# A fused four-layer graph network on one core: stacked keys, staging and value products of the attention layer rewritten

## The reference

```python
Q = (x @ Wq + bq).reshape(Bs, Ns, 4, 32)          # K and V alike
scores = einsum('bnhd,bmhd->bhnm', Q, K) / sqrt(32)
scores = scores + (1.0 - adj[:, None, :, :]) * -1e9
attn = softmax(scores, axis=-1)
out = einsum('bhnm,bmhd->bnhd', attn, V).reshape(Bs, Ns, 128)
return out @ Wo + bo
```

## Time and profile before

| | |
|---|---|
| median of three runs | 13284.21 us |
| the profiled execution | 13291.54 us |
| its span (first to last instruction) | 13289.7 us |
| PE, PEld busy | 95%, 47% |
| DVE, ACT busy | 74%, 72% |
| mean granted TensorE clock | 0.972 |
| PE products of the second layer (L1017) | 7128.7 us |

### The profile page before, as it was taken

One profiled execution on the slowest core, in us unless ns is written; L12 is line 12 of the kernel. 1 busy time (PEld: TensorE's weight loads), 2 busy tenths in 40 slices (PEclk: granted clock), 3 DMA queues, 4 the chain that ended last, 5 costly groups with the idle time before them and its releaser, 6 DMA issues.

```text
span 13289.7 us, 251470 instructions
## 1 busy us (share of the span) xinstructions
PE 12572.4 (95%) x110721; PEld 6215.5 (47%) x110721; DVE 9769.1 (74%) x13975; ACT 9628.7 (72%) x8953; POOL 351.3 (3%) x500
## 2 busy tenths in 40 slices
PE   8998999989999899998999989999899998999989
PEld 3333843338433384333843338433384334843348
DVE  4887748877488774887758877588765887658876
ACT  4886748867488664886648866488664886658866
POOL 1000000000000000000000000000000000000000
PEclk9999999999999999999999999999999999999999
DMA  1001210012100121001310013100130001300022
GB/s 71 17 20 45 100 60 17 20 45 104 56 17 20 48 105 52 17 20 48 110 47 18 19 48 117 40 20 17 52 122 32 20 17 52 129 25 20 17 55 87
DMA packets 126941, 647.66 MB, mean 49 GB/s; under 512 B 15264, under 2 KB 49824, under 8 KB 52128
## 3 DMA queue, kind: packets, MB, share of 16 engines
q1 hardware_dynamic: 92688, 420.78, 9.4%
q0 software_dynamic: 20880, 143.66, 2.9%
q10 hardware_dynamic: 12288, 67.13, 2.2%
HBM read 556.01 MB, written 8.39 MB: 42 GB/s over the span
## 4 chain that ended last, share of the span: by engine, by line
PE 88%; DVE 6%; ACTq 2%; DMA 2%; ACT 1%; issue 1%; POOL 0%; SPq 0%; DVEq 0%
PE ps L1017 50%; PE ps L1001 10%; PE ps L1059 8%; PE ps L1072 4%; PE ps L1030 4%; PE ps L1050 3%; PE ps L1189 3%; ACTq L540 2%; PE ps L953 2%; DMA adj_ring<-in_adj 1%; PE ps L1177 1%; DVE E L678 1%; DVE E L679 1%; DVE PT L705 1%; DVE stats L604 1%
## 5 line engine op out<-in xcount | busy, mean ns | idle before, releaser
L1017 PE MATMUL ps<-E,a_win 128*32 128x512 f32 x65536 | 7128.7, 594 | 46.4 <-ACT E L439 34.9
L1017 PEld LDWEIGHTS ps<-E,a_win 128*32 128x32 f32 x65536 | 2114.9, 110 | 4879.7 <-issue 4737.3
L439 ACT ACTIVATE E<-Q,ka 128x2048 f32<-128x2048 f32 x2048 | 4073.1, 1989 | 0.0
L678 DVE TENSOR_SCALAR E<-Q,kd 128x2048 f32<-128x2048 f32 x2048 | 2631.1, 1285 | 1016.5 <-PE ps L1017 982.4
L438 ACT ACTIVATE E<-Q,ka 128x1280 f32<-128x1280 f32 x2048 | 2786.7, 1361 | 810.9 <-PE ps L1017 786.0
L679 DVE TENSOR_SCALAR E<-Q,kd 128x2048 f32<-128x2048 f32 x2048 | 2623.9, 1281 | 0.0
L746 DVE CUSTOM_DVE_ANT_0 T<-ps,adj_ring 128x2048 f32<-128x2048 f32 x512 | 1173.5, 2292 | 231.9 <-PE ps L1050 205.3
L680 DVE TENSOR_SCALAR E<-Q,kd 128x768 f32<-128x768 f32 x2048 | 1258.8, 615 | 0.0
L464 ACT ACTIVATE T<-T,nmin 128x2048 f32<-128x2048 f32 x512 | 1022.0, 1996 | 319.4 <-issue 199.3
L374 ACT ACTIVATE PT<-ps 128x512 f32<-128x512 f32 x1792 | 999.7, 594 | 287.3 <-PE ps L1059 275.4
L1059 PE MATMUL ps<-ident,T 128*128 128x128 f32 x8192 | 1129.8, 281 | 10.1 <-ACT PT L374 5.9
(11 more groups left out here) (119 smaller groups left out, 7558.4 us busy)
## 6 DMA issues: line engine op xcount, KB each, us to landing
adj_ring<-in_adj SPq DMA_DIRECT2D x384, 1024.0 KB, 4.9
adj_res<-in_adj POOLq DMA_DIRECT2D x128, 1024.0 KB, 7.4
qst<-qh ACTq DMA_DIRECT2D x64, 256.0 KB, 7.9
qst<-ql ACTq DMA_DIRECT2D x64, 256.0 KB, 9.0
kst<-kh ACTq DMA_DIRECT2D x64, 256.0 KB, 5.7
kst<-kl ACTq DMA_DIRECT2D x64, 256.0 KB, 5.9
HW<-in_x POOLq DMA_DIRECT2D x9, 1024.0 KB, 13.3
X<-in_x SPq DMA_DIRECT2D x128, 64.0 KB, 2.0
```

Of the source, the lines that this page charges most:

```text
L439: nc.scalar.activation(E[:, s + 3, :], Q2[:, :], ACT.Relu, bias=ka[:, u, 48 + m:49 + m]).then_inc(e_act, 1)
L678: nc.vector.tensor_scalar(E[:, s, :], Q2[:, :], kd[:, u, m:m + 1], 0.0, ALU.add, ALU.max)
L1017: last = mm(ps[QROWS * grp:QROWS * (grp + 1), 4 * u + c, :], win, E[:, s + grp, c * CH:(c + 1) * CH], start=(m == 0), stop=(m == QUADS - 1 ...
```

## The change

- **Stacking by PE.** The weights of Q and K are loaded four times side by side (`wq_r`, `wk_r`: head h's 32 columns repeated on 128), so one product gives head h's keys on all four partition groups (`fill`). ACT writes the rounded (high) value to all of them, and DVE overwrites the groups that shall hold the low part with the difference (`low`). The 32 staging DMAs of a batch are gone. Only tiles 0 and 1 of the queries are made that way. For tiles 2 to 15, Q is formed once (high part in `AGG`, low part in `HT`) and SP stacks each tile by 16 DMAs of 16 KB (`stack_queries`), two to four tiles ahead.
- **Order.** 28 `fill`s go through PSUM banks 4 to 7 and the first four steps' scores stand between them.
- **Values.** A step takes one quarter (4 key blocks) of all four heads of a tile, instead of all 16 blocks of one head. The four heads' products stand on the four column groups and accumulate in one bank, so nothing is left to combine. The probabilities of a tile are therefore transposed when its four heads are done: group `q` in step `q + 5`. Three banks (4, 5, 6) rotate.
- **Output.** For each tile, DVE spreads the reciprocal sums, PE transposes them (`spread2`), DVE multiplies them onto the result (`attend2`), PE multiplies by `Wo` (`output2`), DVE adds to `X`, and the statistics, the layer norm and the relu of the fourth layer follow for groups of tiles, all within the loop. POOL folds `dinv` into `rstd`.
- **Constants.** 30 small loads instead of 16 ahead of the first work.

The core of the diff (PE; then SP):

```diff
-            def values2(r, h, g, first):
...
-                for k in range(TPC):
-                    last = mm(ps[HD * k:HD * (k + 1), 6 + h % 2, 0:P], V[:, g * TPC + k, h * HD:(h + 1) * HD],
-                              PT2[:, g, k * P:(k + 1) * P], start=(g == 0), stop=(g == NC - 1),
-                              tile_position=(0, HD * k))
...
-                mm(ps[:, 6 + h % 2, P:P + HD], o4[:, h % 2, :], sel[:, :], start=True, stop=True).then_inc(c2_ps, 1)
...
+            def probs_t2(b, q, h):
+                t, g = q // NC, q % NC
+                if g == 0 and h == 0:
+                    pe.wait_ge(p2_rdy, b * STEPS + (t + 1) * HEADS)
...
+            def values2(b, q):
...
+                for k in range(TPC):
+                    for h in range(HEADS):
+                        last = mm(ps[HD * h:HD * (h + 1), 7, 0:P],
+                                  V[:, g * TPC + k, h * HD:(h + 1) * HD], PT2[:, q % 2, h, k * P:(k + 1) * P],
+                                  start=(g == 0 and k == 0), stop=(g == NC - 1 and k == TPC - 1),
+                                  tile_position=(0, HD * h))
...
+            def step2(b, s):
+                q = s - 5
+                if 0 <= q < GROUPS:
+                    for h in range(HEADS - 1):
+                        probs_t2(b, q, h)
+                if 0 <= q - 1 < GROUPS:
+                    values2(b, q - 1)
+                if 0 <= q < GROUPS:
+                    probs_t2(b, q, HEADS - 1)
+                if s % HEADS == 2 and 0 <= s // HEADS - 2 < NT:
+                    spread2(b, s // HEADS - 2)
+                if s % HEADS == 3 and 0 <= s // HEADS - 2 < NT:
+                    output2(b, s // HEADS - 2)
+                if s < STEPS:
+                    scores2(b, s)
...
+            def stack_queries(b, t):
+                sp.wait_ge(f_free, b * FILLS + 5 * HEADS + NC + t // TPC + 1)
+                if t >= 4:
+                    sp.wait_ge(s2_ps, b * STEPS + (t - 3) * HEADS)
+                for blk, part in enumerate((AGG, HT, AGG, HT)):
+                    for h in range(HEADS):
+                        sp.dma_start(qcur[HD * blk:HD * (blk + 1), t % 4, h, :].bitcast(F32),
+                                     part[HD * h:HD * (h + 1), t * P:(t + 1) * P]).then_inc(q_in[t % 4], 16)
```

## The result

The changed kernel takes 12977.9 us (median of 4 runs, 12970.25 to 12991.6), the kernel before 13285.44 (4 runs, 13282.43 to 13297.99). The ratio is 0.9761 [0.9748, 0.9774]: 2.4% faster. Forecast were 13040 with 12950 to 13180, so the direction and the range hold, and the forecast was 62 us too high.

A forecast was written before the change was run, and what follows sets the result against it. PE was taken to bound the kernel, with 28.06 us waiting for staging. Per batch 42.5 + 15 x 17.03 + 3 + 20.8 = 321.8 instead of 354.8; 13291.5 - 264 + 12 = 13040 us, range 12950 to 13180.

The forecast's parts named there:

- Start, 42.5 per batch: Attention layer's start: from first transposes to the transposes of group 0, 42.5 us without any DMA wait, bounds 41.5 to 46.
- Tile, 17.03: Attention loop: one tile lasts 17.03 us, the same as 4 x 4.265 = 17.06 before.
- The four legs: Loop, round a tile: fourth head's minimum to transposes 4.48, to scores 2.92, to next scores 3.84, by DVE to minimum 5.79.
- The 3 us set aside for the small pieces: Tile's fourth step, where DVE sets the pace: statistics, layer norm, relu and adding `bo`, 3 us per batch.
- The cause of the wait: Loop: a tile's transposes need all four heads' exponentials, 5.86 us against 3.73 of PE work, so PE waits once per tile.
- no new wait: Rival, loop: exponentials done within one PE step, 15.5 us per tile, 185 us less, total 12855; chance 0.08.
- The DVE leg: Ring's last leg, scores to the fourth head's minimum: by DVE with mask, copy and add 5.79 us; by PE 5.57.
- End, 20.8: Attention layer's end: from the transposes of step 65 to the fourth layer's first product, 20.8 us.
- Query DMAs, 0.48 per issue: SP's queue in the loop: 16 DMAs per tile at 0.48 us, 7.7 of a tile's 17 us, taken as covered.
- Constants, 12 once: Kernel start: 14 more constants delay the adjacency loads, 12 us once.
- The clock: Rival, loop: PE at half clock in the step behind the wait, 2.92 us more per tile, total 13390; chance 0.03.
- The others keep their durations: Fourth layer and the other layers: durations unchanged, they only start earlier.

The follow-up runs named there:

- Experiment 2: The kernel before, with the 16 staging DMAs of the keys issued by SP while ACT issues those of the queries: 13377.9 us, ratio 1.0056.
- experiment 7: The kernel before, staging only the first of four partition groups, scores contracting over its 32 partitions without the low parts: 13396.7 us, ratio 1.0083.
- experiment 1: The changed kernel, with PE waiting ahead of a head's first transposes for that head's exponential alone, not all four: 12850.7 us, ratio 0.9659.
- experiment 9: The changed kernel, with DVE making the next tile's mask in the tile's third step instead of its fourth: 12983.9 us, ratio 0.9775.
- Experiment 5: On top of experiment 1, DVE copies the last aggregate's transposes, needed by the fourth layer's first product, ahead of the last normalisations: 12818.9 us, ratio 0.9651.
- experiment 4: The changed kernel, with 32 query DMAs of 8 KB per tile instead of 16 of 16 KB: 13616.1 us, ratio 1.0237.
- 6: On top of Experiment 5, the 16 DMAs of replicated weights and biases moved behind the first batch's `x` loads in SP's queue: 12805.2 us, ratio 0.9642.

## Why the prediction was right, point by point

- **The bound** (PE, and its 28.06 us behind the staging). Right. Experiment 2 shows the staging bound by the DMA engines, and 7 that a quarter of it would have brought only 14 of the 28 us in the second batch, 11.4 in the mean. To gain all of it, the stacking by PE also had to take the scores out from behind the load of the next `x` and its statistics, a second wait which the prediction did not see. Nor was the DMA that ended PE's wait the last one, as the prediction read it: ACT issued further ones until 2965.0, 8 us after the first scores.
- **Start, 42.5 per batch.** 43.8 (41.5 in the last batch, and down to 40.3 in experiment 1, by the clock at the start). DVE's new form took 0.76 alone and 0.69 in a row instead of 0.62, inside the bounds 0.57 and 0.8.
- **Tile, 17.03.** This is the term with the largest miss. Without a piece of the statistics or the layer norm in its fourth step a tile took 16.65; with one, 16.90. The four legs, priced at 4.48, 2.92, 3.84 and 5.79, took 4.46, 2.86, 3.94 and 5.64 in the tile shown, and its DVE leg holds such a piece of 0.26: without it 5.38. The rows were read as lengths, but from start to start the pieces are shorter (mask 1.14, copy 0.58, add 0.20), and from the scores to the minimum are 1.22 instead of 1.38. The output product, priced as 0.46, took 0.22 from its start to that of the scores. PE's wait, put at 1.5, is 1.31 and stands 120 times. The 3 us set aside for the small pieces were the right pieces, but came to half: six times 0.25. Together 251.8 instead of 258.5, 6.7 per batch too much.
- **The cause of the wait.** Shown by experiment 1, which takes it away and saves 127 us. The rival "no new wait", 12855, was rightly given a small chance for the code as it stands; experiment 1 makes it the case and measures 12850.7. That the two agree within 5 us is partly luck: the tile was 15.6, not 15.5, and the start and the end differ from their prices.
- **The DVE leg.** Present: 0.26 us more or less on it moves the tile by 0.25. But "5.57 by PE" as the alternative beside 5.79 was too narrow a comparison: experiment 9 shows that the two neighbouring legs share DVE's work, and shortening one lengthens the other.
- **End, 20.8.** 21.8. The list of pieces was right, but the normalisation of three blocks and both relus, 1.4 us, stand ahead of the copies on DVE. Experiment 5 shows that this order, not the dependency, cost 2.4 us per batch.
- **Query DMAs, 0.48 per issue.** Too low: 0.63 in the median, 0.68 in the mean. They are covered, as forecast, with 11 of 16.9 us used; landing takes 2.7 and 2.2 us against 2.0. The warning of the Trainium skill's page "DMA: Bandwidth & Descriptors", section Bandwidth, about small transfers did not bite at 16 KB, and in experiment 4, at 8 KB, the number of issues bound, not the bytes.
- **Constants, 12 once.** 10.1 (first product at 57.14 instead of 47.05).
- **The clock.** 0.98 over the layer instead of 0.92, 1.00 in the loop: no half clock behind a wait of 1.3 us. At the start half the clock was there, as the prediction had it: 0.61 over the first 16 us.
- **"The others keep their durations."** Nearly. From a batch's first product to the attention layer's first transposes all eight batches took 9579.2 us instead of 9588.9, and the fourth layer 817.5 instead of 808.9. Two small errors of opposite sign cancel. No experiment was aimed at the fourth layer, and yet it took 779 to 825 us in sum over the eleven traces, so an agreement of the total to better than some 20 us is luck.
- **The sum.** The gap of 48 us between forecast and profiled execution is 45 from the attention layer, 10 from the layers ahead of it and 2 from the constants, less 9 in the fourth. Of the 45, 34 are the second batch's 317.5 against 321.8, eight times; 11 come from taking the second batch for all (354.8 where the mean was 355.6, and 317.5 where it was 317.0).

What the clock did in these stretches, by the rows: in seven of eight batches of the changed kernel the second layer's last block of 32 products ran at full clock (3.81 us; in two of eight before, else 5.4 to 5.5). The layers ahead are then 2 us shorter, but the first scores of the attention layer come 18.5 us behind the transposes instead of 16.3, so most of it is given back. At the start of the fourth layer the same idle time of 2.79 us led to both clocks in the changed kernel:

```profile
1573.43 3.81 PE L1362 MATMUL ps<-AGG,H 128*128 128x128 f32 x32 [2.79 <-issue]
```

This is the first batch, with a granted clock of 1.00; in the second the same 32 products took 6.70 us at 0.50. Five batches had 3.81, one 5.44 and two 6.7. With 0.40 us of idle time (experiments 5 and 6) all 16 batches had 3.81, and in the kernel before, with 3.35 to 4.6, none of eight. So the idle time just ahead does not decide it alone.

What stays open: what else decides that clock, and with it why the layers ahead became 1.2 us shorter per batch. No experiment varied this alone.

## What to carry to other kernels

A wait for "all of a group", where work is taken piece by piece, costs what the last piece lacks. Here one line, moved into the loop over heads, was worth some 130 us beside the 308 of the whole rewriting. Before pricing a cover or a leg of a ring, ask what is next behind it: the kernel before had a second bound 0.14 us below its loop step and a second wait in the middle of its staging, and each took half or more of what a single removal promised. In this kernel small DMAs cost by their number on the issuing queue (experiment 4), large ones by the time of the DMA engines (experiment 2). A second queue did not help the large ones; whether it would help the small ones was not tried.

## What the runs showed of the hardware

- On SP one SBUF-to-SBUF DMA followed the last after 0.63 us in the median, with 16 KB and with 8 KB alike (mean 0.68 and 0.67), against 0.48 for the 64 KB loads of `x`.
- Staging from SBUF to SBUF went at about 215 GB/s from one queue and from two, with all 16 DMA engines busy (239 and 233 GB/s with the load of `x` beside it).
- At a change of the array's form PE stood idle for 0.17 to 0.36 us each time, also when only the number of contracted rows changed (experiment 7). There the step with products over a quarter of the rows was 0.395 us longer than that with products over all.
- DVE's three-operand instruction on 64 partitions and 512 columns from PSUM takes 0.69 us in a row, no less than the two-operand addition on 128 partitions (0.62).
- Behind the same 2.79 us of idle time TensorE's granted clock, over the next 3 us, was 1.00 in five batches, 0.50 in two and 0.70 in one.
